# A gated attention and mixture-of-experts block: tile steps written out, result rings of sixteen, no cleared tile before sixteen row scatters

## The reference

```
x = x + tanh(g0) * cross_attention(ctx, layernorm(x), mask)      # 8 heads of 16
n = layernorm(x)
scores = sigmoid(n @ gate.T + bias)                              # 9 experts
two best experts per token, their scores divided by their sum -> cw
for e in range(9):
    h = silu(n @ w1[e].T) * (n @ w3[e].T)                        # hidden size 352
    out += cw[:, e] * (h @ w2[e].T)
x = x + tanh(g1) * out
```

## Time and profile before

| what | value |
|---|---|
| median of 3 runs | 225.47 us (224.35 to 226.18) |
| the profiled execution's own time | 226.1 us |
| its span, first to last instruction | 223.8 us |
| mean granted TensorE clock | 0.983 |
| TensorE matmuls busy | 207.0 us, 93% of the span |
| VectorE, ScalarE, GpSimd busy | 66%, 63%, 60% |

### The profile page before, as it was taken

The page is one execution under the profiler, slowest core; times in us unless marked ns, Lnnn a source line. Parts: engine busy times, 40 slices in busy tenths (PEclk is TensorE's granted clock), DMA queues, the critical chain, the costliest instruction groups (busy, mean ns, idle before and its releaser), DMA issues.

```text
span 223.8 us, 5950 instructions
## 1 busy us (share of the span) xinstructions
PE 207.0 (93%) x1618; PEld 166.2 (74%) x1618; DVE 148.1 (66%) x523; ACT 142.0 (63%) x398; POOL 134.2 (60%) x246
## 2 busy tenths in 40 slices
PE   8999995999999999899889899979999997999892
PEld 3677653567666676566559698969999996999892
DVE  0459999477889679888776988334434433434963
ACT  2275869887897877678646666646666655676200
POOL 5228647024322787578678888888888876546210
PEclk9999999799999999999997999999999999999999
DMA  6999999999960000001137332223222221270293
GB/s 175 359 372 242 403 401 405 409 401 312 350 189 1 25 27 24 24 27 37 40 83 202 87 95 62 60 72 80 80 74 58 64 65 39 62 231 32 63 372 130
DMA packets 23598, 34.88 MB, mean 156 GB/s; under 512 B 2561, under 2 KB 15878, under 8 KB 23442
## 3 DMA queue, kind: packets, MB, share of 16 engines
q1 hardware_dynamic: 20610, 29.27, 39.3%
q0 software_dynamic: 2240, 4.23, 5.7%
q10 hardware_dynamic: 720, 1.02, 1.5%
HBM read 15.85 MB, written 19.06 MB: 156 GB/s over the span
## 4 chain that ended last, share of the span: by engine, by line
PE 55%; DVE 14%; POOL 14%; ACT 5%; issue 5%; DMA 5%; SPq 1%; POOLq 0%; ACTq 0%; DVEq 0%
PE pt_ps L1352 9%; POOL x_rows L591 7%; PE score_ps L1165 5%; DMA ctx_r<-in_ctxT 4%; PE score_ps L1310 4%; PE pt_ps L1361 4%; PE ps_a L1215 4%; PE score_ps L1311 3%; PE score_ps L1312 3%; POOL spare L569 3%; PE pt_ps L1203 3%; PE ps_b L1272 2%; DVE less L823 2%; ACT probs L398 2%; PE score_ps L1115 2%
## 5 line engine op out<-in xcount | busy, mean ns | idle before, releaser
L611 POOL DMA_INDIRECT y_rows<-probsT,ids x38 | 37.7, 992 | 12.7 <-ACT probsT L470 6.2
L398 ACT ACTIVATE probs<-score_ps,less 128x128 f32<-128x128 f32 x128 | 37.6, 409 | 0.4 <-DVE less L823 0.4
L591 POOL DMA_INDIRECT x_rows<-stage,slot x32 | 32.6, 1018 | 8.0 <-POOL spare L569 4.5
L1352 PE MATMUL pt_ps<-w,probsT 128*128 x234 | 33.0, 277 | 3.7 <-ACT probsT L477 3.3
L1352 PEld LDWEIGHTS pt_ps<-w,probsT 128*128 128x128 f32 x234 | 30.6, 191 | 5.2 <-issue 5.0
L470 ACT ACTIVATE probsT<-pt_ps,xg 128x128 f32<-128x128 f32 x38 | 14.0, 368 | 30.0 <-PE pt_ps L1352 21.9
L1039 DVE TENSOR_TENSOR xg_low<-ps_a,xg_high 128x128 fp32r<-128x128 f32 x40 | 11.6, 291 | 30.3 <-ACT xg_high L452 17.7
L1310 PE MATMUL score_ps<-w_high,xg_low 128*128 x80 | 29.8, 372 | 0.3
L1048 DVE TENSOR_TENSOR probs<-probs,score_ps 128x352 f32<-128x352 f32 x40 | 20.8, 521 | 10.2 <-PE score_ps L1312 3.0
L1312 PE MATMUL score_ps<-w_high,xg_high 128*128 x80 | 26.3, 329 | 0.0
L1311 PE MATMUL score_ps<-w_low,xg_high 128*128 x80 | 26.2, 327 | 0.0
(11 more groups left out here) (178 smaller groups left out, 457.0 us busy)
## 6 DMA issues: line engine op xcount, KB each, us to landing
x_rows<-pads SPq DMA_DIRECT2D x1, 9945.0 KB, 36.0
w_low<-in_w13T SPq DMA_DIRECT2D x3, 1056.0 KB, 11.6
xg<-x_rows SPq DMA_DIRECT2D x40, 65.0 KB
ctx_r<-in_ctxT SPq DMA_DIRECT2D x4, 512.0 KB, 7.5
y_rows<-pads SPq DMA_DIRECT2D x1, 2048.0 KB, 15.3
w<-in_w2T SPq DMA_DIRECT2D x1, 1728.0 KB, 9.8
kheads<-y_rows SPq DMA_DIRECT2D x3, 512.0 KB, 5.2
mask_b<-in_mask SPq DMA_DIRECT2D x4, 256.0 KB, 8.2
```

Source lines behind the costliest of these rows:

```text
L398: last = nc.scalar.activation(probs[:, r % 2, h, :], score_ps[:, r % 2, h, :], ACT.Exp, bias=less[:, r % 2, h:h + 1])
L591: pool.indirect_dma_start(x_rows[:, :], bass.IndirectOffsetOnAxis(ap=slot[:, par, c, p:p + 1], axis=0), stage[:, par, c, p, :], None, boun ...
L611: pool.indirect_dma_start(y_rows[:, :], bass.IndirectOffsetOnAxis(ap=ids[:, r:r + 1], axis=0), yt[:, r, :], None, bounds_check=last_row, o ...
L1352: last = nc.tensor.matmul(into[:, 0:D], hidT[:, q3, c, :], w2[:, bass.ds(e3, 1), c, :].rearrange("p o d -> p (o d)"), start=(c == 0), stop ...
```

## The change

It makes the rings `yt`, `ids_in` and `ids` sixteen places long (`YR`), with sixteen semaphores `st_y`; `yt` moves into the memory of `vals`, whose last reader is the attention loop. ScalarE now waits for the scatter of t-16, VectorE for GpSimd's id copy of t-16, and GpSimd waits for the scatter of t-16 before that copy. It writes out all steps on ScalarE, VectorE and SyncE. It drops `space(3 * D)` ahead of the sixteen scatters of groups three and four. On TensorE each expert's number is taken out once, a step before its first use, behind the `hidden` matmuls, and the `reg_load` moves there too. SyncE waits at the end for sixteen places. The last sums read `yt` at the new places. The core of the diff (left out: places where only a test for a loop register falls away, the semaphore list and the last sums' index):

```diff
 NT = 2 * NB + NE - 1
-TR = 8
+TR, YR = 8, 16
 PARTS = [slice(0, 4), slice(4, 8), slice(8, 12), slice(12, 14), slice(14, 16)]
...
         pads = sb("pads", [P, NE, RW])
-        ids_in = sb("ids_in", [P, TR], I32)
-        xg, xg_high, xg_low, ids, zero = sb("xg", [P, TR, RW]), sb("xg_high", [P, 2, P], F32R), sb("xg_low", [P, 2, P], F32R), sb("ids", [P, TR], I32), sb("zero", [P, 1], I32)
+        ids_in = sb("ids_in", [P, YR], I32)
+        xg, xg_high, xg_low, ids, zero = sb("xg", [P, TR, RW]), sb("xg_high", [P, 2, P], F32R), sb("xg_low", [P, 2, P], F32R), sb("ids", [P, YR], I32), sb("zero", [P, 1], I32)
...
         hidT = flat[1][:, 0:2 * NC * P].rearrange("p (r c t) -> p r c t", r=2, c=NC)
-        yt = flat[1][:, 2 * NC * P:2 * NC * P + TR * D].rearrange("p (r d) -> p r d", r=TR)
+        yt = vals[:].rearrange("p b h d -> p (b h d)")[:, 0:YR * D].rearrange("p (r d) -> p r d", r=YR)
...
-        def tile_turns(eng, step, between):
-
-            for k in range(sum(EARLY)):
+        def tile_turns(step, between):
+
+            for k in range(NT + 3):
                 step(k, k % TR, k // TR)
                 between(k)
-            with eng.Fori(sum(EARLY) // TR, NT // TR) as i:
-                for r in range(TR):
-                    step(i * TR + r, r, i)
-            for k in range(NT, NT + 3):
-                step(k, k % TR, k // TR)
...
-            return not isinstance(k, int) or 0 <= k - lag < NT
+            return 0 <= k - lag < NT
...
                 sp.wait_ge(st_last[p], 32)
-            with sp.Fori(len(EARLY), NT // TR) as i:
-                for r in range(TR):
-                    sp.wait_ge(ids_cast, i * TR + (r + 1 - TR))
-                    sp.wait_ge(y_done, i * TR + (r + 1 - TR))
-                    row = sp.value_load(row_of[0:1, bass.ds(i * TR + r, 1)], min_val=0, max_val=NE * CAP)
-                    sp.dma_start(xg[:, r, :], x_rows[bass.ds(row, P), :]).then_inc(ld_tile[r], 16)
+            for t in range(sum(EARLY), NT):
+                sp.wait_ge(ids_cast, t + 1 - TR)
+                sp.wait_ge(y_done, t + 1 - TR)
+                row = sp.value_load(row_of[0:1, t:t + 1], min_val=0, max_val=NE * CAP)
+                sp.dma_start(xg[:, t % TR, :], x_rows[bass.ds(row, P), :]).then_inc(ld_tile[t % TR], 16)
...
             sp.dma_start(xs[:], out_tok).then_inc(x2_back, 16)
-            for r in range(TR):
-                sp.wait_ge(st_y[r], (NT // TR - (1 if r >= TR - SUMMED else 0)) * 16)
+            for place in range(YR):
+                sp.wait_ge(st_y[place], len(range(place, NT - SUMMED, YR)) * 16)
             y_tok = y_rows.rearrange("(p n c) d -> p n c d", p=P, c=2)
...
                     act.wait_ge(x_turned, k + 1)
-                    if not isinstance(k, int) or k >= 2:
+                    if k >= 2:
                         act.wait_ge(h3_mm, k - 1)
...
                     act.wait_ge(h1_mm, t + 1)
-                    if not isinstance(t, int) or t >= 2:
+                    if t >= 2:
                         act.wait_ge(hid_done, t - 1)
...
-                if isinstance(k, int) and k == SWITCH - 1:
+                if k == SWITCH - 1:
                     turned_back(NB + 2)
...
                     act.wait_ge(y_mm, t + 1)
-                    if not isinstance(k, int) or t >= TR:
-                        act.wait_ge(st_y[place], turn * 16)
-                    nc.scalar.activation(yt[:, place, :], bank[1 if is_last(t) else 5][:, 0:D], ACT.Copy, scale=xg[:, place, C_WEIGHT:C_WEIGHT + 1]).then_inc(y_done, 1)
+                    if t >= YR:
+                        act.wait_ge(st_y[t % YR], t // YR * 16)
+                    nc.scalar.activation(yt[:, t % YR, :], bank[1 if is_last(t) else 5][:, 0:D], ACT.Copy, scale=xg[:, place, C_WEIGHT:C_WEIGHT + 1]).then_inc(y_done, 1)
...
                     act.wait_ge(hid_turned, t + 1)
-                    if not isinstance(t, int) or t >= 2:
+                    if t >= 2:
                         act.wait_ge(y_mm, t - 1)
...
                 for c in copies:
-                    if g >= NG - 2:
-                        space(3 * D)
                     pool.indirect_dma_start(x_rows[:, :], bass.IndirectOffsetOnAxis(ap=slot[:, par, c, p:p + 1], axis=0), stage[:, par, c, p, :], None,
...
             def tile(k, r):
+                s = k % YR
                 pool.wait_ge(ids_cast, k + 1)
-                nc.gpsimd.tensor_tensor(ids[:, r:r + 1], ids_in[:, r:r + 1], zero[:], ALU.add).then_inc(ids_copied, 1)
+                if k >= YR:
+                    pool.wait_ge(st_y[s], k // YR * 16)
+                nc.gpsimd.tensor_tensor(ids[:, s:s + 1], ids_in[:, s:s + 1], zero[:], ALU.add).then_inc(ids_copied, 1)
                 pool.wait_ge(ids_copied, k + 1)
...
                 pool.wait_ge(y_done, k + 1)
-                pool.indirect_dma_start(y_rows[:, :], bass.IndirectOffsetOnAxis(ap=ids[:, r:r + 1], axis=0), yt[:, r, :], None,
-                                        bounds_check=last_row, oob_is_err=False).then_inc(st_y[r], 16)
+                pool.indirect_dma_start(y_rows[:, :], bass.IndirectOffsetOnAxis(ap=ids[:, s:s + 1], axis=0), yt[:, s, :], None,
+                                        bounds_check=last_row, oob_is_err=False).then_inc(st_y[s], 16)
...
                 dve.wait_ge(ld_tile[place], turn * 16 + 16)
-                if not isinstance(t, int) or t >= TR:
-                    dve.wait_ge(st_y[place], turn * 16)
-                nc.vector.tensor_copy(ids_in[:, place:place + 1], xg[:, place, C_ID:C_ID + 1]).then_inc(ids_cast, 1)
+                if t >= YR:
+                    dve.wait_ge(ids_copied, t + 1 - YR)
+                nc.vector.tensor_copy(ids_in[:, t % YR:t % YR + 1], xg[:, place, C_ID:C_ID + 1]).then_inc(ids_cast, 1)
...
             def tile(k, r, i):
-                if r == 0:
-                    unpacked.clear()
                 if has(k, 0):
-                    if r % PACK == PACK - 1:
-                        if r == TR - 1 and i < len(EARLY):
-                            pe.wait_ge(table_set, i + 2)
-                        unpack_next(i, r // PACK + 1)
                     pe.wait_ge(ld_tile[r], i * 16 + 16)
-                    if not isinstance(k, int) or k >= 1:
+                    if k >= 1:
                         pe.wait_ge(x_low, k)
...
                     t, q = k - 1, (r - 1) % 2
-                    e = expert(r - 1)
+                    e = expert_of(k - 1)
                     pe.wait_ge(x_low, t + 1)
-                    if not isinstance(t, int) or t >= 2:
+                    if t >= 2:
                         pe.wait_ge(hid_done, t - 1)
...
                     hidden(bank[2 + q], q, e, 1).then_inc(h3_mm, 1)
-                if isinstance(k, int) and k == SWITCH - 1:
+                if has(k, 0):
+                    if r % PACK == PACK - 1:
+                        if r == TR - 1 and i < len(EARLY):
+                            pe.wait_ge(table_set, i + 2)
+                        unpack_next(i, r // PACK + 1)
+                    expert_of(k)
+                if k == SWITCH - 1:
                     turn_rows(NB + 2)
...
                     t3, q3 = k - 3, (r - 3) % 2
-                    e3 = expert(r - 3)
+                    e3 = expert_of(k - 3)
                     into = bank[5]
...
                         pe.wait_ge(hid_copied, t3 + 1)
-                        if not isinstance(t3, int) or t3 >= 1:
+                        if t3 >= 1:
                             pe.wait_ge(y_done, t3)
```

More of the change, by code:

```diff
@@ L173, in build @@
         st_last = [sem(f"st_last{n}") for n in range(UN)]
-        st_y = [sem(f"st_y{n}") for n in range(TR)]
+        st_y = [sem(f"st_y{n}") for n in range(YR)]
         ld_y = [sem(f"ld_y{n}") for n in range(len(PARTS))]
@@ L240, in in_switch @@
         def in_switch(k):
-            return isinstance(k, int) and k == SWITCH
+            return k == SWITCH
         def is_last(t):
-            return isinstance(t, int) and t == NT - 1
+            return t == NT - 1
         @block.sync
@@ L483, in between @@
                     nc.scalar.preload_act_table(ACT.Silu)
-            tile_turns(act, tile, between)
+            tile_turns(tile, between)
             for u in range(BY_PE[0]):
@@ L1036, in tile @@
                     dve.wait_ge(x_high, k + 1)
-                    if not isinstance(k, int) or k >= 2:
+                    if k >= 2:
                         dve.wait_ge(h3_mm, k - 1)
                     nc.vector.tensor_tensor(xg_low[:, r % 2, :], bank[6][:, 0:P], xg_high[:, r % 2, :].bitcast(F32), ALU.subtract).then_inc(x_low, 1)
-                if isinstance(k, int):
-                    within(k)
+                within(k)
                 if has(k, 1):
@@ L1051, in tile @@
                     turn = i if r >= 3 else i - 1
-                    if not isinstance(t, int) or t < NT - SUMMED:
+                    if t < NT - SUMMED:
                         cast_ids(t, place, turn)
@@ L1078, in between @@
```

(22 more changed lines are left out.)

## The result

The median after is 218.8 us (218.01 to 218.95, four runs) against 224.91 us before; the ratio is 0.973, 95% interval 0.969 to 0.977. That is one half of the result. The changed kernel was timed again on three more Trainium2 chips: the ratio was 0.974 on two of them, and **238.3 us against 227.9, ratio 1.046** (1.044 to 1.048), on the third. The first half comes first here, the other under chips D, C and E.

What follows compares the result with a forecast made beforehand. The prediction took TensorE's 2.07 us steps from step 15 on, plus one ring wait, as the bound. From the median 225.5 us it took 1.80 for the ring and 0.5 for expert numbers: 223.2 us, range 221.0 to 225.6.

Steps and rivals of the forecast that it cites:

- The ring's wait, and who ends it: Step 14 to 15: result 10 waits for result 2's scatter, queued behind GpSimd's eight last-group scatters, to free its ring place.
- So the ring costs 3.87 - 2.07 = 1.80 us: TensorE's step holding the ring wait takes 3.87 us against the usual 2.07; a ring of sixteen gains 1.80 us.
- The two don't add: Dropping the memsets before GpSimd's scatters alone would remove nearly the same 1.80 us as the longer ring; its added value is 0.
- the margin of 2.6 us: Loads of tile 16, issued at 147.61, stay ahead of its turn, expected at 150.24 with the longer ring.
- The gap of 0.49 us: Between GpSimd scatters without memsets: gap between 0 and 0.49 us, taken as 0.49, so a pitch of 1.47 instead of 1.69.
- From step 15 on the floor is 2.07 us: In the later tile steps TensorE's 2.07 us per step bounds; lighter VectorE, ScalarE or SyncE work gains nothing.
- expert numbers -0.5: TensorE's register work moved behind the previous step's matmuls: gains 0.5 us of 0.6 excess, bounds -0.7 to +0.3.
- Side effect on VectorE, net 0: Steps 3 to 11: denser scatters but no memsets change small VectorE operations by -1.2 to +2.8 us, taken as 0.
- Writing out, zero: Tiles written out on ScalarE, VectorE and SyncE remove registers and branches from engines with slack: 0 us.
- The loops' rival: Loops on ScalarE, VectorE and SyncE cause the slow steps 31 to 33; writing out gives 221.2 us, chance 0.22.
- the odd stretch: Steps 31 to 33 take 6.10 us for two, 1.96 us lost, seen once, cause unknown; the forecast left it in.
- The slower rival: Eight unbroken last-group scatters shut VectorE out, up to 10.2 us with some 2 covered: 231 us, chance 0.07.

Runs made afterwards that it cites:

- D: Chip with its own group of runs: kernel before 226.8 us; kernel before without the last group's memsets 234.5 us, ratio 1.035; with two memsets there 231.6 us.
- C: Chip with its own group of runs: kernel before 224.2 us; changed kernel, again, 218.9 us, ratio 0.974; kernel before without the last group's memsets 220.8 us.
- E: Chip with its own group of runs: kernel before 227.9 us; changed kernel, again, 238.3 us; changed kernel with the old order of expert numbers 238.6 us.
- A: Chip with its own group of runs, the kernel before (224.2 us) with one edit each: no sixteen memsets 219.4 us; new expert-number order 224.0; tiles written out 224.1.
- B: Chip with its own group of runs, the changed kernel (218.6 us) with one part undone: ring of eight 219.4 us; memsets back 220.2; old expert-number order 217.8.

## Why the prediction was right and wrong

- *The ring's wait, and who ends it*: right. GpSimd's row of last-group scatters ends it, and both edits, each alone, take it away.
- ***"So the ring costs 3.87 - 2.07 = 1.80 us"*: the step that failed**, a term mis-sized. It was read from an execution in which half a clock at 117 to 120 us had made TensorE late, and a late TensorE waits less. The wait ends at a time of its own. Over steps 14 to 18 it costs 2.0 us behind a half-clock stretch (repeated kernel before), 3.6 without one, and 4.6 where a half-clock stretch follows its idle time. Removing it gave 4.4 to 5.2 us in the median (either edit alone, A to C) and 2.5 us between two executions with the same half-clock stretch ahead. That the median lies at the dear end is shown; the share of each case is not.
- *"The two don't add"*: nearly right. 4.7 to 5.2 us for the memsets, 4.4 for the ring, 5.4 to 6.0 for both. With the ring alone, the loads of tiles 16 to 18 are late by 0.97 us: the margin of 2.6 us that I gave them was read behind the late TensorE too (there, tile 16 would be turned 3.1 us sooner than I had it, and its load is issued only 2.1 us sooner).
- *The gap of 0.49 us*: wrong, 0.30, inside its bounds of 0 to 0.49. Result 2's scatter came at 139.65, not 143.5, of which 2.5 us are the slots that came sooner (129.11 for 131.6) and 1.4 the pitch.
- *From step 15 on the floor is 2.07 us*: right; expert numbers -0.5, measured 0.5 in the steps and nothing that the time shows. (The excess over 2.07 us in the earlier trace rows was 0.47 + 0.22 = 0.7 us, where I had 0.6.)
- *Side effect on VectorE, net 0*: without the memsets the two small operations fell from 0.50 and 0.67 us to at most 0.18 and 0.21 on A, B and C, and steps 7 to 12 from 11.09 to 10.52. The memsets are not all of that: written out, but with them, these steps took 10.71. The Trainium skill (SBUF — State Buffer, "SBUF: two separate sides"), that VectorE's two-port operations and GpSimd exclude each other for a whole instruction, would let denser scatters stretch such operations more. They shrank, and in the profile of after L923 runs in 0.15 us from 130.54, wholly inside the scatter of 130.38, so this scatter did not exclude it, and it is not the share of time in scatters that sets it. On A, B and C over 0.25 us was seen only in kernels with the memsets; on D and E the first took 0.38 to 0.40 in the three without any. What stretches them is open.
- *Writing out, zero*: right (0.998). The loops' rival is dead: the odd stretch is absent in loops too. The Trainium skill (Runtime: NRT & Kernel Launch, "Instruction fetch mechanics"), that a taken branch stalls for a fetch, gave no time here that the run could show.
- *The odd stretch, kept in the forecast*: wrong for A to C, where no kernel has it, changed or not. It was a visit of the late signals, 1.98 us of the difference between the two profiles, though not of that between the medians on one chip; I had named it unexplained and left it in.
- *The slower rival, 231 us, chance 0.07*: it came true on E at 238.3 us (and on D at 237.5 with a ring of eight), and, as far as the coincidence in time shows, by the mechanism's first half, scatters in an unbroken row shut another engine's progress out. But its victim was TensorE's signals, not VectorE, and its argument against ("a gap of 0.49 us remains") was no protection at 0.30.

## What to carry to other kernels

A wait that is ended by something other than the waiting chain is an anchor: price it from the time at which it ends against the earliest time at which the chain can come, over several executions, never as one step's excess; and count a gain ahead of it as nothing. Before two traces are compared, look at a row that should not depend on the kernel (here how many of the scatters' landings the record holds, and waits put down to "remote"), and time a change that makes one engine's instructions denser on more than one chip. No version here was shown to be faster than before on both kinds of chip. The obvious candidate, the ring of sixteen with the memsets back (220.2 us on B, ratio 0.982), never ran on D or E. The changed kernel with the old order of expert numbers was not told from the changed one on B or on E.

## What the runs showed of the hardware

- GpSimd's indirect scatters of 128 rows with nothing between come 1.27 us apart: 0.97 and a gap of 0.30. A memset of 128x384 bf16 between makes it 1.69, two 2.21.
- On two chips of five, while such scatters follow each other unbroken, TensorE's signals came 5 us late, in order and 0.05 us apart, and single waits for them took up to 6.0 us; the changed kernel took 4.6% more on E. With a memset in between, none came late in those stretches. With only a copy of 0.20 us in between, a scatter each 1.5 us, they came up to 1.6, 2.1 and 2.6 us late in three profiles.
- At each idle time of TensorE of 4.1 us and more (D and E) its clock stood at half before the idle time was over or within 1.1 us behind it, for 3.4 to 13.7 us. Of two idle times of 2.8 us, one was followed by 3.4 us at half clock (tiles written out) and one was not (new order of expert numbers). The half-clock stretches near 116 us had no such idle time ahead.
